# A mixture-of-experts kernel on one core: seven products also for batch 0's routed pairs, weight sums ahead of the gate and up pieces

## What is computed

```
x = x + _L0_cond_ref(x, cond_8, weight, mask, bias)      # w_bot = sum_g y[b,g] * weight[g] * mask; x @ w_bot + bias
# for each batch: the two largest of softmax(cond_8), renormalised
g = jnp.einsum('bsh,hi->bsi', x, gate_w)                 # 256 -> 1024
u = jnp.einsum('bsh,hi->bsi', x, up_w)
h = jax.nn.gelu(g, approximate=True) * u
out = we * jnp.einsum('bsi,ih->bsh', h, down_w)          # 1024 -> 256; two routed experts
x = x + out + _gemma_mlp(x, shared_gate, shared_up, shared_down)
```

## Time and profile before

| | us |
|---|---|
| median of 3 runs | 421.45 |
| lowest, highest | 421.34, 422.14 |
| the profiled execution | 421.95 |
| its span, first to last instruction | 420.1 |
| mean granted TensorE clock in it | 0.999 |

### The profile page before, as it was taken

How to read it: one execution, slowest core, us unless ns; L and a number is a source line. 1 busy time by engine, 2 the same in 40 slices (tenths; PEclk the granted TensorE clock), 3 DMA queues, 4 the chain that set the end, 5 groups by cost and what they waited for, 6 DMA issues and landing times.

```text
span 420.1 us, 7010 instructions
## 1 busy us (share of the span) xinstructions
PE 412.1 (98%) x2133; PEld 351.7 (84%) x2133; DVE 259.5 (62%) x452; ACT 235.6 (56%) x448; POOL 264.6 (63%) x275
## 2 busy tenths in 40 slices
PE   8999999999999999999999999999999999999997
PEld 6688888888878888888888888788888888888886
DVE  3556643243348776765767877567666666665595
ACT  5665455454435476656555656656555556665641
POOL 1565465388602279989724848998860857898820
PEclk9999999999999999999999999999999999999999
DMA  7664234234111422342110153222310042231011
GB/s 255 224 197 116 84 97 129 77 101 124 52 25 34 132 89 75 98 127 79 51 27 0 48 176 96 79 75 75 100 25 25 0 126 75 77 116 61 25 25 52
DMA packets 20187, 36.24 MB, mean 86 GB/s; under 512 B 2242, under 2 KB 3010, under 8 KB 20162
## 3 DMA queue, kind: packets, MB, share of 16 engines
q1 hardware_dynamic: 19872, 35.66, 28.0%
q10 hardware_dynamic: 290, 0.26, 0.2%
HBM read 33.82 MB, written 2.10 MB: 85 GB/s over the span
## 4 chain that ended last, share of the span: by engine, by line
PE 55%; POOL 18%; issue 17%; ACT 4%; DVE 3%; DMA 1%; SPq 1%; POOLq 0%; DVEq 0%; ACTq 0%
POOL eg_lo L1193 7%; PE g_ps L504 6%; PE o_ps L556 6%; PE g_ps L505 6%; PE g_ps L508 6%; PE u_ps L505 6%; PE u_ps L508 6%; PE u_ps L504 6%; PE o_ps L563 5%; PE p_ps L563 4%; POOL s_raw L1203 3%; PE l_ps L463 2%; DMA l_raw<-l_w 1%; POOL s_raw L1206 1%; POOL ed_lo L1234 1%
## 5 line engine op out<-in xcount | busy, mean ns | idle before, releaser
L1193 POOL TENSOR_TENSOR eg_lo<-raw_g,eg_hi 128x512 fp32r<-128x512 f32 x64 | 83.9, 1326 | 61.4 <-ACT eg_hi L711 61.4
L1000 DVE SCALAR_TENSOR_TENSOR u_ps<-gelu,route_cur,u_ps 128x512 f32<-128x512 f32 x64 | 48.3, 755 | 80.5 <-PE u_ps L508 45.5
L740 ACT ACTIVATE gelu<-g_ps 128x512 f32<-128x512 f32 x96 | 57.4, 598 | 48.9 <-PE g_ps L508 48.6
L504 PE MATMUL g_ps<-x_hi,eg_hi 128*128 128x512 f32 (+1 forms) x128 | 50.9, 397 | 2.9 <-ACT gelu L740 2.9
L505 PE MATMUL g_ps<-x_hi,eg_lo 128*128 128x512 f32 (+1 forms) x128 | 50.4, 394 | 0.0
L504 PE MATMUL u_ps<-x_hi,eg_hi 128*128 128x512 f32 (+1 forms) x128 | 49.9, 389 | 0.0
L505 PE MATMUL u_ps<-x_hi,eg_lo 128*128 128x512 f32 (+1 forms) x128 | 49.8, 389 | 0.0
L1036 DVE TENSOR_TENSOR h_lo<-t_raw,h_hi 128x1024 fp32r<-128x1024 f32 x34 | 43.6, 1283 | 4.3 <-ACT h_hi L767 4.3
L762 ACT CAST h_hi<-u_ps 128x512 fp32r<-128x512 f32 x34 | 20.0, 588 | 39.5 <-DVE u_ps L1000 20.7
L995 DVE TENSOR_TENSOR u_ps<-gelu,u_ps 128x512 f32<-128x512 f32 x32 | 22.3, 696 | 31.1 <-PE u_ps L508 30.1
L508 PE MATMUL g_ps<-x_lo,eg_hi 128*128 128x512 f32 (+1 forms) x128 | 39.6, 390 | 0.0
(11 more groups left out here) (234 smaller groups left out, 1131.8 us busy)
## 6 DMA issues: line engine op xcount, KB each, us to landing
raw_g<-experts SPq DMA_DIRECT2D x64, 256.0 KB, 2.8
raw_d<-experts SPq DMA_DIRECT2D x32, 256.0 KB, 2.8
l_raw<-l_w SPq DMA_DIRECT2D x8, 256.0 KB, 5.8
x_in<-xT SPq DMA_DIRECT2D x8, 256.0 KB, 4.4
raw_g<-shared SPq DMA_DIRECT2D x8, 256.0 KB, 4.3
raw_d<-shared SPq DMA_DIRECT2D x8, 256.0 KB, 3.0
outT<-out_sb SPq DMA_DIRECT2D x6, 256.0 KB, 3.2
mask<-l_mask SPq DMA_DIRECT2D x2, 128.5 KB, 5.8
```

The source lines that it names most:

```text
L504: pe.matmul(ps, w_hi[:, at:at + P], x1_at(x1_hi, b, hh), start=(hh == 0), stop=False)
L740: act.activation(gelu[:, s % 2], g_ps[:], ACT.Gelu_apprx_tanh).then_inc(gelu_done, 1)
L1000: dve.scalar_tensor_tensor(u_ps[:, s % 2], gelu[:, s % 2], route_cur[:, k:k + 1], u_ps[:, s % 2], ALU.mult, ALU.mult).then_inc(h_done, 1)
L1193: pool.tensor_tensor(eg_lo[:, j % RING], raw_g[:, j % RAW_G], eg_hi[:, j % RING].bitcast(F32), ALU.subtract).then_inc(gu_lo_done, 1)
```

## The change

- `fast` now also holds for batch 0 from pair 4 on (its eight routed pairs). Their down product takes the seven products, with the sums of weights and hidden blocks that go with them. The shared pairs of batch 0 stay plain, their 512 output columns in `o_ps`.
- POOL's order in a step: `expert_s` stands ahead of the two `split_gu`. In batch 0 the gate and up pieces of steps 8 to 19 are now split two in an odd step.
- The four shared sums go to the end: `shared_s(0)` at step 21 of batch 0, `shared_s(1)` at step 23, `shared_s(2)` and `shared_s(3)` after it, where ACT casts them between the first two steps of batch 1. SP's loads stand in an order to match.
- Batch 0's output goes the way of batches 1 and 2. P5 moves beside P1 in PSUM; `o_ps[:, 0]` is copied to `out_sb` directly, not to `s_raw`. With that `s_raw` no longer waits for the output sums.
- In the last batch DVE adds P2 and P3 first, then P4, P6, P7, P5, and P1 last; `final_down` waits for seven of these additions, not six.

```diff
-            return not at_first(b) and not (at_last(b) and p >= LAST_FAST)
+            return not (at_first(b) and p < PAIRS) and not (at_last(b) and p >= LAST_FAST)
...
-                product(P6, wt, None, S2, T2, first, False)
-                product(P7, wt, None, S3, T3, False, last)
-                product(P4, wt, None, A22, T4, first, False)
-                product(P5, wt, None, S1, T1, False, last).then_inc(down_done, 1)
+                product(P5, wt, S1, T1, False, last)
+                product(P6, wt, S2, T2, p == 0 or first_fast(b, p), False)
+                product(P7, wt, S3, T3, False, last)
+                product(P4, wt, A22, T4, p == 0, last).then_inc(down_done, 1)
...
                 if s == STEPS - FINAL:
-                    pe.wait_ge(rest_done, 6)
+                    pe.wait_ge(rest_done, 7)
...
                     activate(b + 1, 0)
-                    if not at_first(b):
-                        split_t(b, NP - 1)
+                    split_t(b, NP - 1)
                     split_b11(b + 1, 0)
-                    if not at_first(b):
-                        evacuate_123(b)
+                    evacuate_23(b)
+                    if at_first(b):
+                        split_shared_s(2)
                     activate(b + 1, 1)
                     split_b2(b + 1, 0)
-                    if not at_first(b):
-                        evacuate_4567(b)
+                    evacuate_1567(b)
+                    if at_first(b):
+                        split_shared_s(3)
...
-                dve.tensor_tensor(out_flat, x1_all(b).rearrange("p (q c) -> p q c", c=TH), P1.unsqueeze(1).to_broadcast([P, 4, TH]), ALU.add).then_inc(rest_done, 1)
-                dve.wait_ge(rest_done, 1)
-                dve.tensor_tensor(out_sb[:, 0], out_sb[:, 0], o_ps[:, 0], ALU.add).then_inc(rest_done, 1)
+                dve.tensor_tensor(out_sb[:, 0], x1_at(x1, b, 0), o_ps[:, 0], ALU.add).then_inc(rest_done, 1)
...
+                dve.tensor_tensor(out_flat, out_flat, P1.unsqueeze(1).to_broadcast([P, 4, TH]), ALU.add).then_inc(rest_done, 1)
...
-                    if s >= STEPS - 2 * PAIRS + 1 and s % 2:
-                        shared_s((s - STEPS + 2 * PAIRS - 1) // 2)
-                    if s < SPLIT_LEAD + ECH:
-                        split_gu(0, s - SPLIT_LEAD)
+                    if s == STEPS - 3:
+                        shared_s(0)
+                        split_shared_s(0)
+                    if s == STEPS - 1:
+                        shared_s(1)
+                        split_shared_s(1)
+                    q = (s - CHUNKS + 1) // 2
+                    if s % 2 and 0 <= q < EPR:
+                        expert_s(0, q)
...
+                for i in (2, 3):
+                    shared_s(i)
+                    split_shared_s(i)
+                sum_products(0)
...
                         split_d(b, (s - CHUNKS) // 2)
+                    q = (s - CHUNKS + 1) // 2
+                    if s % 2 and 0 <= q < EPR and fast(b, PAIRS + q):
+                        expert_s(b, q)
                     if s % 2 and s < 2 + ECH:
                         split_gu(b, s - 3)
                         split_gu(b, s - 2)
-                    q = (s - CHUNKS + 1) // 2
-                    if s % 2 and 0 <= q < EPR and fast(b, PAIRS + q):
-                        expert_s(b, q)
```

More of the change, by code:

```diff
@@ L124, in build @@
         x_flat = x_in[:].rearrange("p h t -> p (h t)")
[L125 removed]
+        stage_15, stage_67 = x_flat[:, 0:T], x_flat[:, T:2 * T]
+        stage_1, stage_5 = stage_15[:, 0:TH], stage_15[:, TH:T]
         out_flat = out_sb[:].rearrange("p h t -> p (h t)").rearrange("p (q c) -> p q c", c=TH)
@@ L304, in expert_of, with store @@
                 return sp.value_load(top_idx[0:1, bass.ds(b, 1), k], min_val=0, max_val=E - 1)
+            def store(b):
+                for hh, sums in ((0, SUMS - 1), (1, SUMS)):
+                    sp.wait_ge(sum_done, SUMS * b + sums)
+                    sp.dma_start(outT[bass.ds(b, 1), :, hh].rearrange("a p t -> (a p) t"), out_sb[:, hh]).then_inc(stored, 16)
             def batch_0():
@@ L342, in batch_0 @@
                     load_gu(1, j, n)
-                for hh in range(HH):
-                    sp.wait_ge(out_done, hh + 1)
-                    sp.dma_start(outT[0, :, hh], out_sb[:, hh]).then_inc(stored, 16)
+                store(0)
             def batch(b, with_next):
@@ L381, in batch @@
                         load_gu(b + 1, j, n)
-                    for hh, sums in ((0, SUMS - 1), (1, SUMS)):
-                        sp.wait_ge(sum_done, SUMS * (b - 1) + sums + 1)
-                        sp.dma_start(outT[bass.ds(b, 1), :, hh].rearrange("a p t -> (a p) t"), out_sb[:, hh]).then_inc(stored, 16)
+                    store(b)
                 else:
@@ L556, in plain_down, with product @@
                         mm = pe.matmul(psums[oh], block_of(w, blk), x, start=(first and i == 0), stop=(last and i == 2))
-                    if last and oh == 0:
-                        mm.then_inc(sum0_done, 1)
                 mm.then_inc(down_done, 1)
-            def product(ps, wt, ht, blk, hf, first, last):
+            def product(ps, wt, blk, hf, first, last):
                 for i, (w, h) in enumerate(((0, 0), (0, 1), (1, 0))):
@@ L568, in products_123 @@
                 pe.wait_ge(h_lo_done, STEPS * b + 2 * p + 2)
-                if p == 0:
+                if first_fast(b, p):
                     pe.wait_ge(x1_done, HH)
-                    pe.wait_ge(out_done, 1)
-                    pe.wait_ge(evac_done, 4 * b)
-                first, last = p == 0, p == (LAST_FAST - 1 if at_last(b) else NP - 1)
+                elif p == 0:
+                    pe.wait_ge(evac_done, 3 * b - 1)
+                last = p == (LAST_FAST - 1 if at_last(b) else NP - 1)
                 wt = d_weights(p)
-                product(P1, wt, None, A11, B11, first, last)
-                product(P2, wt, None, A12, B21, first, False)
-                product(P3, wt, None, S4, B22, False, last).then_inc(down_done, 1)
+                product(P1, wt, A11, B11, p == 0 or first_fast(b, p), False)
+                product(P2, wt, A12, B21, p == 0, False)
+                product(P3, wt, S4, B22, False, last).then_inc(down_done, 1)
             def products_4567(b, p):
@@ L615, in down @@
                 elif at_first(b):
-                    plain_down(b, s, [o_ps[:, oh] for oh in range(HH)], s == 0, s == STEPS - 1)
+                    plain_down(b, s, [o_ps[:, oh] for oh in range(HH)], s == 0, False)
                 elif s < STEPS - FINAL:
@@ L754, in split_b11 @@
                 act.copy(h_hi[:, 0:TH], u_ps[:, 0, 0:TH]).then_inc(h_hi_done, 1)
-                if not (isinstance(b, int) and b == 1 and p == 0):
+                if not first_fast(b, p):
                     act.wait_ge(t_done, 4 * pair_count(b, p))
@@ L788, in weights_beside @@
                         split_shared_d(PAIRS - 1)
-                    if SPLIT_LEAD <= s < SPLIT_LEAD + ECH:
+                    if SPLIT_LEAD <= s < CHUNKS:
+                        split_gu(0, s - SPLIT_LEAD)
+                    if CHUNKS <= s < SPLIT_LEAD + ECH and s % 2:
+                        split_gu(0, s - SPLIT_LEAD - 1)
                         split_gu(0, s - SPLIT_LEAD)
@@ L1142, in batch @@
                     form_t234(b + 1, 0)
-                    if at_first(b):
-                        for oh in range(HH):
-                            store_ready_0(oh)
-                    else:
-                        add_p4(b)
+                    add_p4(b)
                 else:
```

144 lines of the change are left out of this document (63 added, 81 removed).

## The result

| | before | changed |
|---|---|---|
| median, us (five runs each) | 421.45 | 419.02 |
| lowest, highest | 421.30, 422.14 | 417.98, 419.37 |
| profiled execution | 421.95 | 419.19 |
| its span | 420.1 | 417.2 |

The ratio is 0.9938, with a 95% interval of 0.9922 to 0.9953. The kernel is faster by 2.4 us (0.6%), not by the forecast 4.5 us, and its median of 419.02 lies above the range, which ended at 418.6.

What follows compares the result with a forecast made beforehand. PE, busy 98% of the span, was taken as the bound, with 5.05 us of holds behind late gelu. Terms -5.05 - 1.28 + 1.4 + 0.45 = -4.5 us took the median from 421.45 to 416.9 us, range 415.0 to 418.6.

Steps and rivals of the forecast that it cites:

- Part 1: Batches 1 to 3: POOL's sums ahead of gate and up pieces remove PE's holds; -5.05 us, bounds -5.05 and -3.
- Part 2: Batch 0: seven products take eight routed pairs from 8.16 to 8.00 us each; -1.28 us.
- The rule of the Trainium skill: Batch 0's down products: weight loads and matmuls both set spacing, making seven products 0.49 us dearer per pair, +3.9 us.
- Part 3: Change from batch 0 to 1: PE held 0.9 and 0.5 us by late shared sums; +1.4 us, bounds 0 and +3.
- the shared trips: Change of batches: each runs POOL sums 1.8 us, ACT's cast 0.62, `sd_lo` 1.29, with 0.1 of handing over.
- the output sums at 0: Batch 1's first steps: `sum_products(0)`, seven POOL operations, costs 0 because batch 2 stands the same work without a hold.
- the lock: POOL's first sum takes 1.44 us instead of 0.46 while DVE runs an all-SBUF operation; about 1.0 per pair.
- Part 4: End of batch 3: P1's later addition delays the last split, so PE waits; +0.45 us, bounds 0.2 and 0.7.
- The trips being dearer: `x_lo` pairs or change of batches: holds stay or shared round trips cost more; 418.5 us, chance 0.22.
- Hidden trips: Change of batches: the shared sums' round trips hide and cost PE nothing; 415.5 us, chance 0.20.
- The lock twice on a routed round: Seven-product pairs: two DVE meetings make POOL's round 8.5 us, which then sets the pace; 425 us, chance 0.03.
- Pace by weight loads: Batch 0's seven products: loads set the pace, 0.74 us more per pair; 424.1 us, chance 0.01.

Runs made afterwards that it cites:

- the order alone: Kernel before, with POOL forming the weight sums ahead of the two gate and up pieces in batches 1 to 3: 416.84 us, 416.65 us when repeated.
- experiment 5: Changed kernel, DVE's subtraction for the low part of T cut to 8 of 1024 columns in batch 0's last three routed pairs: 417.05 us.
- experiment 4: Changed kernel, the seven POOL operations summing batch 0's output cut to 8 of every 256 columns: 418.54 us.
- experiments 3: Changed kernel, POOL's weight sums of the shared pieces cut to 8 of 128 columns: 415.66 us.
- experiment 7: Changed kernel, two of the four shared sums formed in steps 5 to 7 of batch 0, casts and loads moved to match: 415.69 us.
- experiment 6: Changed kernel, DVE adds P1 in the last batch behind step 22's multiplication instead of ahead of it: 418.47 us.
- experiment 8: Changed kernel, two shared sums at batch 0's start and P1 added behind step 22's multiplication in the last batch: 415.29 us.
- experiment 9: Changed kernel with POOL's old order: 426.31 us. Repeats: kernel before with new order, 416.65; changed kernel with early shared sums and later P1, 415.18.

## Why the prediction missed

**Part 1, right in mechanism and size.** Forecast -5.05 us; the order alone moved the span by 5.1, and PE's starts in batches 1 to 3 by 5.06. No round of batches 1 to 3 is held, the `x_lo` pairs among them.

**Part 2, right.** Forecast -1.28. The pairs are 8.00 us apart from the first on: steps 8 to 20 of batch 0 take 50.72 us instead of 51.68, 0.16 for each of six pairs. With the costs of parts 3 and 4 taken away, the kernel stands 1.47 us below the order alone on the same chip (415.18 and 416.65). The rule of the Trainium skill that I weighed there would have cost time; it did not. (Its 98 ns lie on a straight line between the two figures, not halfway.)

**Part 3, the step that failed: the length of the shared trips, and the output sums at 0.** The chain of waits was right, its size wasn't: forecast +1.4 us, measured +3.1. PE takes 27.38 us where three seven-product pairs want 24.00, so 3.38 us are lost; the kernel before lost 0.28 between the same steps itself (24.60 us, where two plain pairs and one of seven products want 24.32), and the difference is 3.10. With that the parts add up to -5.05 - 1.28 + 3.10 + 0.48 = -2.75 us, and the profiled executions differ by 2.76. The forecast's own clock against the trace, zero at ACT's L748 at 101.76, in us:

| | forecast | measured |
|---|---|---|
| shared sums 0 formed | 5.2 | 5.4 |
| `sd_lo` 0 | 7.2 | 7.5 |
| routed sums, with the lock | 10.0 | 10.4 |
| last `ed_lo` | 13.5 | 13.9 |
| shared sums 1 | 15.3 | 15.9 |
| PE goes on | 16.6 | 17.2 |
| `sd_lo` 1 | 17.3 | 18.0 |
| shared sums 2, with the lock | 20.1 | 21.0 |
| PE goes on again | 21.4 | 22.4 |

The first mis-sized term is the chain's many small steps. I took four sums at 1.79 us and let each group start at once; in the trace they take 1.84 and begin 0.14 after the subtraction ahead of them has ended (`ed_lo` to 115.68, the sums from 115.82). That is 0.19 for each group: three groups make 0.57 of the 0.6 us by which the first hold's end was missed, four make 0.76 of the 1.0 of the second; the rest are hand-overs. The locks themselves were forecast at the right places and size (1.0 each, and experiment 5 has 1.96 for the two). The 1.7 us that part 3 was short by are these:

- The first two holds are 1.35 and 0.90 us instead of 0.9 and 0.5, so 0.85 more. Since the chain has no slack, each 0.1 in it is 0.1 of PE. A wait that just fails to be hidden is the worst place for a rounding.
- The third hold, forecast as none, is 0.26. The fourth cast began 0.37 us after its sums had ended (sum to 126.79, cast at 127.16); the others began 0.08 or 0.09 after. The same 0.37 stands in experiment 5. What it is, no run here tells.
- `sum_products(0)` was priced at 0 with the argument that batch 2 stands the same work. It cost about 0.4 us (experiment 4; the rest of the 0.47 is slower matmuls behind the third hold). Its POOL operations meet L1033 of batch 1's first pair, and this time DVE is the one that waits. In experiments 3 and 7 the subtraction meets them too (2.02 and 1.52 us) without a loss: there it starts 0.87 us behind batch 1's first down product, here 2.26. The cost shows only on top of a chain already late.
- 0.40 us are slower first matmuls, for which the forecast had no term, and 0.28 that the kernel before lost itself come off.

Together 1.35 + 0.90 + 0.26 + 0.47 + 0.40 = 3.38 us, less 0.28. The low bound of 0, if the lock misses both sums, was wrong as well: in experiment 5 it misses both, and 1.42 us stay. The high bound of +3 for this part was fair; what was wrong was to keep a chance of only 0.22 for dearer trips and to end the range at their middle. 0.3 us more of the miss come from the medians: the profiled executions differ by 2.76 us, the medians by 2.43.

**Part 4, right.** Forecast +0.45. The end of the span is 11.95 us behind step 20's down product instead of 11.47, so +0.48, and experiment 6 takes it back. The list of waits shows 0.2 us of it only. (One slip in its working changes nothing: 414.38 + 0.69 + 0.9 is 415.97, not 415.95.)

**The rivals.** The trips being dearer is what happened, and its 418.5 was the nearest of the times given. Hidden trips: they would have been 415.5, and with experiment 7 they are hidden, at 415.7. The lock twice on a routed round: no pair is the longer for it. Pace by weight loads: not seen, all pairs at 8.00.

The best version is experiment 8: 415.29 us there and 415.18 in experiment 9, 3.7 to 3.8 below the changed kernel.
